# Delta stage of a two-layer AdaLN kernel: 48 projected columns spread over the heads, in place of 768

## The reference, cut to what matters

```
q, k, v = (x @ Wq), (x @ Wk), (x @ Wv)            # 16 heads x 16
beta = sigmoid(x @ Wbeta + b_beta)                 # one value per head
vsum = v.sum(-1)                                   # one value per head
h_t = beta_t * h_(t-1) + k_t * vsum_t              # per head, 16 values (all columns j of k alike in h)
o_t = q_t.sum(-1) * h_t                            # only the sum of q over a head matters
y = x + o @ Wo + b_o ;  out = ln_g * normalise(y) + ln_b
```

## Time and profile before

| | |
|---|---|
| median of 3 runs | 2445.0 us |
| the profiled execution | 2444.07 us |
| its span | 2442.4 us (1.67 us lie around it) |
| PE / DVE / ACT / POOL busy | 2070.8 / 1827.2 / 1274.5 / 700.0 us |
| `phase_delta`, first matmul to the first of the next phase | 1745.46 to 1932.10 us |

### The profile page before, as it was taken

One profiled execution on the slowest core, in us unless ns is written; L12 is line 12 of the kernel. 1 busy time (PEld: TensorE's weight loads), 2 busy tenths in 40 slices (PEclk: granted clock), 3 DMA queues, 4 the chain that ended last, 5 costly groups with the idle time before them and its releaser, 6 DMA issues. The chain is left out here.

```text
span 2442.4 us, 39942 instructions
## 1 busy us (share of the span) xinstructions
PE 2070.8 (85%) x10413; PEld 881.0 (36%) x10413; DVE 1827.2 (75%) x2427; ACT 1274.5 (52%) x1553; POOL 700.0 (29%) x1073
## 2 busy tenths in 40 slices
PE   5886888888889988888888889578799597999996
PEld 4441222222222122222222221456454254677775
DVE  2886999989999989999899999458589642333332
ACT  0555888878888878888788888122212210111110
POOL 0563111111111121111111111037356566133334
PEclk8898999999999999999999999789899798999998
DMA  3453221203121222212030000440000033344442
GB/s 118 131 173 98 38 36 20 28 12 50 20 30 18 28 43 39 29 20 28 24 82 19 15 3 0 142 148 30 1 0 0 6 110 118 98 105 101 106 95 26
DMA packets 124640, 133.71 MB, mean 55 GB/s; under 512 B 35258, under 2 KB 118931, under 8 KB 123793
## 3 DMA queue, kind: packets, MB, share of 16 engines
q1 hardware_dynamic: 109904, 117.96, 19.6%
q0 software_dynamic: 14592, 14.08, 3.1%
HBM read 96.95 MB, written 50.63 MB: 60 GB/s over the span
## 5 line engine op out<-in xcount | busy, mean ns | idle before, releaser
L914 DVE SCALAR_TENSOR_TENSOR arena<-ps_s,arena 128x1024 f32<-128x1024 f32 (+3 forms) x1152 | 1229.1, 1128 | 85.2 <-ACT arena L886 62.8
L886 ACT ACTIVATE arena<-ps_s 128x1024 f32<-128x1024 f32 (+3 forms) x1152 | 1043.3, 951 | 280.8 <-PE ps_s L792 266.3
L792 PE MATMUL ps_s<-arena 128*128 128x512 bf16 (+3 forms) x2304 | 645.4, 369 | 152.8 <-DVE arena L914 98.3
L817 PE MATMUL ps_o<-arena 128*32 128x512 f32 (+3 forms) x4608 | 578.2, 574 | 16.7 <-POOL arena L950 16.2
L792 PEld LDWEIGHTS ps_s<-arena 128*128 (+1 forms) x2304 | 174.2, 97 | 841.1 <-issue 709.2
L945 POOL COPY arena<-values 128x64 f32 x576 | 134.3, 236 | 878.6 <-PE ps_o L817 865.5
L1934 ACT ACTIVATE arena<-g_ps_g 128x320 f32<-128x320 f32 (+1 forms) x96 | 41.9, 436 | 315.6 <-PE g_ps_u L1866 315.6
L2130 POOL DMA_INDIRECT out<-values,slot_ids x80 | 123.4, 1542 | 247.4 <-DVE values L2081 215.6
L2054 DVE TENSOR_TENSOR arena<-g_ps_u,arena 128x320 f32<-128x320 f32 (+1 forms) x96 | 47.1, 491 | 165.3 <-ACT arena L1934 165.3
L817 PEld LDWEIGHTS ps_o<-arena 128*32 128x32 f32 x4608 | 91.2, 108 | 197.6 <-issue 144.7
L950 POOL TENSOR_SCALAR_AFFINE_SELECT arena<-arena 128x512 f32<-128x512 f32 x128 | 81.2, 634 | 241.8 <-DVE arena L914 241.8
(11 more groups left out here) (208 smaller groups left out, 1943.3 us busy)
## 6 DMA issues: line engine op xcount, KB each, us to landing
arena<-parts_dram SPq DMA_DIRECT2D x320, 64.0 KB, 3.0
parts_dram<-arena SPq DMA_DIRECT2D x32, 384.0 KB, 3.2
arena<-parts_dram SPq DMA_DIRECT2D x24, 512.0 KB, 7.1
slots_in_dram<-in_empty_slots SPq DMA_DIRECT2D x10, 1040.0 KB, 19.7
arena<-slots_in_dram SPq DMA_DIRECT2D x16, 650.0 KB, 5.9
arena<-in_L_ffn_w_gate SPq DMA_DIRECT2D x16, 352.0 KB, 3.1
arena<-in_L_ffn_w_up SPq DMA_DIRECT2D x16, 352.0 KB, 3.5
arena<-in_L_attn_x SPq DMA_DIRECT2D x8, 512.0 KB, 3.6
```

The lines of the kernel that those rows point to most:

```text
L792: last = pe.matmul(ps_s[:, (2 * step.slot + pair) % 3, h, step.w0:], m.k_stack[:, bass.ds(head, 1), bass.ds(step.kt * P, P)].rearrange("p ...
L817: last = pe.matmul(ps_o[32 * h:32 * h + 32, step.j % 2, step.w0:], v_pad[:, step.slot, h], probs[:, step.slot, h, step.w0:], start=step.fi ...
L886: act.activation(probs[:, step.slot, 2 * pair:2 * pair + 2, step.w0:], ps_s[:, (2 * step.slot + pair) % 3, :, step.w0:], ACT.Exp, scale=1. ...
L914: dve.scalar_tensor_tensor(p, ps_s[:, (2 * step.slot + pair) % 3, :, step.w0:], 0.0, p, ALU.not_equal, ALU.mult).then_inc(bank, 1)
```

## The change

In `phase_weights` the six copies over the columns go. Instead one narrow matrix `l1_narrow` of 96 columns is filled: v sums at 0 to 15, Wbeta at 32 to 47 (loaded there), q sums at 64 to 79, zeros between. A constant 0/1 matrix `spread`, loaded from memory, maps 16 heads to 256 channels, once in each group of 32 partitions. `b_beta` is loaded in another layout.

In `phase_delta` the narrow product is made once for a block, copied out by three ScalarE instructions on 32 partitions each (the middle one with the sigmoid), and spread to 128 channels by three matmuls of 32 rows each, at three row positions of the array, for each half. The products for the keys are as before. All of the scan's TensorE work moves one step later. The scan reads beta from PSUM. The second normalisation goes from VectorE to ScalarE, with GpSimd giving -mean/deviation as its offset.

```diff
@@ LayerNorm
+    def scale_and_offset(self, pool, b, s):
+        hold(self.m, pool, self.mvs, b + 1)
+        pool.tensor_scalar(self.ve[:, s], self.mv[:, s, :, 1], EPS, None, ALU.add).then_inc(self.added, 1)
+        pool.tensor_scalar(self.offset[:, s], self.mv[:, s, :, 0], -1.0, None, ALU.mult).then_inc(self.added, 1)
+        hold(self.m, pool, self.added, 2 * b + 2)
+        pool.tensor_tensor(self.rstd[:, s], self.ve[:, s], self.m.mhalf[:], ALU.pow).then_inc(self.rst, 1)
+        hold(self.m, pool, self.rst, 2 * b + 1)
+        pool.tensor_tensor(self.offset[:, s], self.offset[:, s], self.rstd[:, s], ALU.mult).then_inc(self.rst, 1)
+    def normalise_by_scale(self, act, b, s, tiles):
+        act.wait_ge(self.rst, 2 * b + 2)
+        for t in range(TT):
+            last = act.activation(self.xn[:, s, t], tiles[:, t], ACT.Identity, bias=self.offset[:, s, t:t + 1],
+                                  scale=self.rstd[:, s, t:t + 1])
+        last.then_inc(self.normed, 1)
@@ phase_weights
-            for n, w in enumerate((m.l1_q, m.l1_v)):
-                link(dve.tensor_reduce(sums[:, n], w.rearrange("p k (h d) -> p k h d", d=DH), AX.X, ALU.add))
-            for k in range(KC):
-                for src, w in ((sums[:, 0, k], m.l1_q), (sums[:, 1, k], m.l1_v), (m.beta_narrow[:, k], m.l1_beta)):
-                    dve.tensor_copy(w[:, k].rearrange("p (h d) -> p h d", d=DH),
-                                    src.rearrange("p (h a) -> p h a", a=1).to_broadcast([P, NH, DH]))
+            for at, w in ((64, m.l1_q), (0, m.l1_v)):
+                link(dve.tensor_reduce(m.l1_narrow[:, :, at:at + NH], w.rearrange("p k (h d) -> p k h d", d=DH), AX.X, ALU.add))
+                link(dve.memset(m.l1_narrow[:, :, at + NH:at + 32], 0.0))
+            link(dve.memset(m.l1_narrow[:, :, 32 + NH:64], 0.0))
@@ phase_delta, TensorE
+            def project_narrow(b, s, h):
+                pe.wait_ge(k_copied, 2 * b + 1)
+                for k in range(KC):
+                    last = pe.matmul(ps_k[0:96], m.l1_narrow[:, k], m.h_odd[:, k, bass.ds(b * BT, BT)], start=k == 0, stop=k == KC - 1)
+                last.then_inc(n_done, 1)
+            def project_keys(b, c):
+                if c == 0:
+                    pe.wait_ge(n_copied, 3 * b + 3)
+                else:
+                    pe.wait_ge(k_copied, 2 * b + 2)
...
+            def spread(b, c):
+                pe.wait_ge(n_copied, 3 * b + 3)
+                pe.wait_ge(q_used, 2 * b + c + 1)
+                for row, (ps, heads) in enumerate(((ps_v, narrow), (ps_b, decay), (ps_q, narrow))):
+                    at = 32 * row
+                    last = pe.matmul(ps[:, :], m.spread[at:at + 32, c], heads[at:at + 32], start=True, stop=True, tile_position=(at, 0))
+                last.then_inc(spread_done, 1)
-            pipeline(pe, [(0, lambda b, s, h: project(b, 0)), (1, out), (0, lambda b, s, h: project(b, 1)),
-                          (3, lambda b, s, h: ln2.transposes(pe, b, s))])
+            pipeline(pe, [(1, lambda b, s, h: project_keys(b, 0)), (1, lambda b, s, h: spread(b, 0)),
+                          (1, lambda b, s, h: project_keys(b, 1)), (2, out), (1, lambda b, s, h: spread(b, 1)),
+                          (0, project_narrow), (4, lambda b, s, h: ln2.transposes(pe, b, s))])
@@ ScalarE
+            def take_narrow(b, s, h):
+                act.wait_ge(n_done, b + 1)
+                act.wait_ge(spread_done, 2 * b)
+                act.activation(narrow[0:32], ps_k[0:32], ACT.Copy).then_inc(n_copied, 1)
+                act.activation(decay[32:64], ps_k[32:64], ACT.Sigmoid, bias=m.b_beta[32:64, 0:1]).then_inc(n_copied, 1)
+                act.activation(narrow[64:96], ps_k[64:96], ACT.Copy).then_inc(n_copied, 1)
-            pipeline(act, [(0, take), (3, modulate)])
+            def normalise(b, s, h):
+                act.wait_ge(ln2.turned, b + 1)
+                act.wait_ge(rows_done, b + 1)
+                ln2.normalise_by_scale(act, b, s, m.x[:, bass.ds(b * TT, TT)])
+            pipeline(act, [(0, take_narrow), (4, modulate), (0, lambda b, s, h: take(b, 0)), (0, lambda b, s, h: take(b, 1)),
+                           (2, normalise)])
@@ VectorE
-                dve.wait_ge(beta_made, n + 2)
-                dve.tensor_tensor_scan(state[:, c], beta[:, c], keys[:, c], start, ALU.mult, ALU.add).then_inc(scanned, 1)
+                dve.tensor_tensor_scan(state[:, c], ps_b[:, :], keys[:, c], start, ALU.mult, ALU.add).then_inc(scanned, 1)
-                           (1, lambda b, s, h: ln1.normalise(dve, b, s, y[s], out=y[s])), (2, normalise)])
+                           (1, lambda b, s, h: ln1.normalise(dve, b, s, y[s], out=y[s]))])
@@ GpSimd
-                            (2, lambda b, s, h: ln2.inverse_deviation(pool, b, s)), (1, gain), (2, rows)])
+                            (2, lambda b, s, h: ln2.scale_and_offset(pool, b, s)), (1, gain), (2, rows)])
```

More of the change, by code:

```diff
@@ L187, in place_weights @@
     a = Carver(m.arena)
-    (m.w_o, m.w_r, m.w_k, m.w_v, m.l1_k, m.l1_q, m.l1_v, m.l1_beta, m.l1_o) = (a.take(KC, D) for _ in range(9))
+    (m.w_o, m.w_r, m.w_k, m.w_v, m.l1_k, m.l1_q, m.l1_v, m.l1_o) = (a.take(KC, D) for _ in range(8))
+    m.l1_narrow = a.take(KC, 96)
+    m.spread = a.take(KC, P)
     m.router = a.take(KC, 32)
@@ L192, in place_weights @@
     m.mu = a.take(2, KC)
-    m.b_beta = a.take(KC)
+    m.b_beta = a.take(1)
     m.ln_gain, m.ln_shift, m.b_o = a.take(D), a.take(D), a.take(D)
     m.router_b = a.take(E_)
-    m.beta_narrow = a.take(KC, NH)
     m.even_at = a.at
@@ L216, in load_weights @@
     for dst, name in ((m.w_o, "woT"), (m.w_r, "W_rT"), (m.w_k, "W_kT"), (m.w_v, "W_vT"), (m.l1_k, "L1_attn_Wk"),
-                      (m.l1_q, "L1_attn_Wq"), (m.l1_v, "L1_attn_Wv"), (m.beta_narrow, "L1_attn_Wbeta"), (m.l1_o, "L1_attn_Wo"),
+                      (m.l1_q, "L1_attn_Wq"), (m.l1_v, "L1_attn_Wv"), (m.l1_narrow[:, :, 32:32 + NH], "L1_attn_Wbeta"), (m.l1_o, "L1_attn_Wo"),
                       (m.router, "router_wide"), (m.s_gate, "L1_ffn_sw_gate"), (m.s_up, "L1_ffn_sw_up")):
@@ L223, in load_weights @@
         load(m.mu[:, k], m.ins[name].rearrange("(k p) -> p k", p=P), allow_slow_non_contiguous=True)
-    load(m.b_beta, m.ins["b_beta_rep"].rearrange("(k p) -> p k", p=P), allow_slow_non_contiguous=True)
+    load(m.b_beta, m.ins["b_beta_narrow"].rearrange("(k p) -> p k", p=P), allow_slow_non_contiguous=True)
+    load(m.spread, m.ins["spread"].rearrange("p (k n) -> p k n", k=KC))
     for dst, name in ((m.ln_gain, "L1_attn_ln_g"), (m.ln_shift, "L1_attn_ln_b"), (m.b_o, "L1_attn_b_o"),
@@ L1157, in __init__ @@
         self.rstd = a.take(2, TT)
+        self.offset = a.take(2, TT)
         if own:
@@ L1209, in sem @@
             return ctx.enter_context(nc.semaphore("w_" + name))
-        sums = Carver(m.arena2).take(2, KC, NH)
         chain, zeroed = sem("chain"), sem("zeroed")
@@ L1509, in phase_delta @@
         keys = a.take(KC, BT)
-        beta = a.take(KC, BT)
+        narrow = a.take(BT)
+        decay = a.take(BT)
         state = a.take(KC, BT)
@@ L1519, in phase_delta @@
         ps_y = pb("ps_y", [P, 2, 2 * D])
-        k_done, v_done, b_done, q_done = sem("k_done"), sem("v_done"), sem("b_done"), sem("q_done")
-        k_copied, v_used, beta_made, q_used = sem("k_copied"), sem("v_used"), sem("beta_made"), sem("q_used")
+        n_done, k_done, spread_done = sem("n_done"), sem("k_done"), sem("spread_done")
+        n_copied, k_copied, v_used, q_used = sem("n_copied"), sem("k_copied"), sem("v_used"), sem("q_used")
         scanned, carried, y_done, y_added, scaled, gained = (sem("scanned"), sem("carried"), sem("y_done"), sem("y_added"),
@@ L1530, in _ @@
             pe.sem_inc(ln2.turned, 2)
[L1532 to L1541, removed]
+            def project_narrow(b, s, h):
[8 more added lines that the diff above has]
+                    pe.wait_ge(k_copied, 2 * b + 2)
+                for k in range(KC):
+                    last = pe.matmul(ps_k[:, :], m.l1_k[:, k, c * P:c * P + P], m.h_odd[:, k, bass.ds(b * BT, BT)],
+                                     start=k == 0, stop=k == KC - 1)
+                last.then_inc(k_done, 1)
+            def spread(b, c):
[5 more added lines that the diff above has]
+                last.then_inc(spread_done, 1)
             def out(b, s, h):
@@ L1559, in _, with take @@
             act.sem_inc(k_copied, 1)
-            act.sem_inc(beta_made, 1)
             act.sem_inc(ln2.taken, 1)
[L1563 to L1570, removed]
+            def take_narrow(b, s, h):
[4 more added lines that the diff above has]
+                act.activation(narrow[64:96], ps_k[64:96], ACT.Copy).then_inc(n_copied, 1)
+            def take(b, c):
+                n = 2 * b + c
+                act.wait_ge(k_done, n + 1)
+                act.wait_ge(scanned, n + 1)
+                act.activation(keys[:, c], ps_k[:, :], ACT.Copy).then_inc(k_copied, 1)
             def modulate(b, s, h):
```

(12 more changed lines are left out.)

## The result

| | before | changed |
|---|---|---|
| median of 6 runs | 2444.04 us (2441.87 to 2447.03) | 2459.28 us (2457.71 to 2464.45) |
| ratio, 95% interval | | 1.0066, 1.0053 to 1.0079 |
| span of the profiled execution | 2442.4 us | 2462.7 us |
| PE / DVE / ACT / POOL busy | 2070.8 / 1827.2 / 1274.5 / 700.0 | 2041.9 / 1784.2 / 1294.1 / 693.8 |
| R(2) to R(7), five periods | 98.2 us | 120.2 us |

R(t) is, as in the prediction, the start of the product with q (L1599, now L1639) of half 0 of block t. TensorE works 28.9 us less, VectorE 43.0 us less, and the kernel is slower. The forecast was 2461 in a range of 2446 to 2478. The profiled execution of the changed kernel is one of its slower ones, 5 us above the median (2464.45).

The account below looks back on a forecast made before the run. VectorE bounds the kernel by a little, TensorE right behind; changed, a ring of waits sets five periods of 23.9 us. +16.3 up to R(7), +0.6 behind it and -0.8 in `phase_weights` give +16.1: 2461 us, range 2446 to 2478.

Parts of the forecast that it names:

- the sum: Whole kernel: +16.3 us up to R(7), +0.6 behind it, -0.8 in `phase_weights`, together +16.1 us.
- DVE, R to the end of the statistics: Each period in `phase_delta`: product with q, residual, add and statistics on VectorE take 7.16 us.
- GpSimd and hand-over to ScalarE: Each period: GpSimd makes the normalisation's scale and offset in 2.30 us, plus 0.12 to hand over.
- PE to R at full clock: Each period on TensorE: keys 1.72, spread 1.07, keys 1.72, `out` to the product with q 3.72 us.
- the low clock: TensorE restarts at 1.2 GHz after waiting 8.7 us for ScalarE, costing 2.4 us in all five periods.
- start of the phase to R(0): Block 0: narrow product 3.54 at low clock, copies 1.69, keys 1.72, spread 1.07, then 2.10 us; R(0) = 1755.9.
- the ring: `phase_delta`, R(t) to R(t+1): one chain of waits over four engines, 21.48 us at full clock, 23.9 with restart.
- The rival in which the engines' loads decide: `phase_delta`: normalisation's inputs come early enough, each engine's own load decides, 2412 us; 12% chance.
- The normalisation and take_narrow on ScalarE: Each period: four normalisations of 0.56 less 0.09 overlap, 1.88 us; three copies of the narrow product, 1.69 us.
- The spread: TensorE, each half: three row tiles run side by side in 1.07 us, bounds 0.43 and 2.57.
- The serial rival: The spread's matmuls run one after the other, +1.5 us for each on the chain, 2476 us; 12% chance.
- The DVE: VectorE, each block: normalisation's 4.66 us go, scan 1.28 for 3.08; 19.63 falls to 13.2 us.

Follow-up runs that it names:

- run 5: Changed kernel with TensorE's pause filled from block 3 on by repeated narrow and throw-away products, transposes first: 2452.78 us, ratio 1.0035.
- run 1: Changed kernel with ScalarE's second normalisation one block later, skew 3 in place of 2: 2431.64 us, ratio 0.9957.
- run 2: Changed kernel with the second normalisation back on VectorE, all else as changed: 2431.95 us, ratio 0.9962.
- run 6: Changed kernel with ScalarE's normalisation and GpSimd's rows at skew 3, and `out` ahead of the second keys on TensorE: 2423.12 us, ratio 0.9911.
- run 4: Changed kernel with the narrow product computed five times over in every block: 2482.91 us, ratio 1.0170.

## Why the prediction was right, point by point

The mechanism was right; that the size came out so close is in part luck. The medians differ by 15.2 us (the ratio makes it 16) where the sum had +16.1. But in the profiled execution of the changed kernel, the only one whose terms can be read, the difference is 20.3 us. The terms are these.

| term | predicted | measured |
|---|---|---|
| DVE, R to the end of the statistics | 7.16 | 7.14 |
| GpSimd and hand-over to ScalarE | 2.42 | 2.48 |
| ACT normalise | 1.88 | 1.98 |
| ACT take_narrow, hand-over | 1.79 | 2.04 |
| PE to R at full clock | 8.23 | 8.46 |
| the low clock | 2.4 | 1.9 |
| period | 23.9 | 24.03 |
| start of the phase to R(0) | 10.4 | 13.7 |
| R(0) to R(2) | 27.7 | 30.8 |
| R(2) to R(7) | 119.5 | 120.2 |
| behind R(7) to the next phase | +0.6 against before | -0.3 |
| `phase_weights`, from its first product (L1226, now L1246) to the next phase | -0.8 | -0.7 (7.2 to 6.5) |

The measured parts of the period are the differences of starts in its timeline; full clock is what the keys (1.92) and the spread (1.06) take in run 5 and in the first periods, with 1.82 and 3.66 for the rest.

From the start of the phase to R(7) that is 164.7 us against 141.4 before, 23.3 more, where the sum had 16.3. With -0.3 and -0.7 it makes +22.3; all else in the kernel took 2.0 us less in this execution, for a reason that wasn't looked for, which gives the +20.3. Of the 7.0 us by which the sum was short up to R(7), the five periods of the ring are only 0.7. The rest lies in the first blocks, 3.3 up to R(0) and 3.1 from there to R(2). The two ends of the period's range, 22.6 and 26, aren't what its bounds add up to (22.2 and 26.7, the spread side by side); the measured period lies in either range.

*The ring.* Right in its mechanism and its members: runs 1 and 2 cut it at different places, and the time fell by 27 us in both; run 1 alters nothing but the order in ScalarE's queue. The rival in which the engines' loads decide is out: even with the ring cut, in run 1, another ring sets the period. Only in run 2 is it a load, VectorE's 17.8 us.

*The normalisation and take_narrow on ScalarE.* 1.98 and 1.89 against 1.88 and 1.69. One normalisation takes 0.59 us and not 0.56; the overlap of 0.09 that I took from L1200 is there (they start 0.50 apart). Among the three copies it is not: of 0.57, 0.68 and 0.59 us, they start 0.59 and 0.71 apart.

*The spread.* Three row tiles run side by side: six instructions in 1.06 us at full clock, 1.07 forecast. The serial rival is out.

*The clock.* It fell at every restart of the ring: the keys take 3.78 us in all five. The cost is 1.9 by the timeline (3.71 less 1.92 for the keys, 1.20 less 1.06 for the spread) and 2.0 by run 5, not 2.4: the level was back within the spread of the same block. So the restart came back in all five periods, as forecast. Where I was off is the start, here in the changed kernel (first three rows) and in run 2:

```profile
1743.29 3.70 PE L1554 MATMUL e_ps_k<-arena 128*96 128x512 f32 x4 [3.36 <-ACTq L1592]
1748.98 3.78 PE L1563 MATMUL e_ps_k<-arena 128*128 128x512 f32 x4 [1.99 <-ACT arena L1600]
1777.67 2.81 PE L1563 MATMUL e_ps_k<-arena 128*128 128x512 f32 x4 [1.99 <-ACT arena L1600]
1738.09 3.70 PE L1554 MATMUL e_ps_k<-arena 128*96 128x512 f32 x4 [3.36 <-ACTq L1592]
1743.78 1.99 PE L1563 MATMUL e_ps_k<-arena 128*128 128x512 f32 x4 [1.99 <-ACT arena L1600]
```

The narrow product of block 0 runs at the low level, as forecast. I counted the first keys behind it at full clock, and they ran low too, as did the first spread and the second keys (granted clock 0.50 to 0.51 up to 1758.30); the keys of block 2 ran partly so. In runs 1, 5 and 6, with the same first blocks, the first keys took 3.78 us as well, and R(0) came 13.6 us after the phase's start in run 1. In run 2 they took 1.99, and R(0) came after 10.9. That may be a part of why executions of the changed kernel lie up to 7 us apart: the traced execution with the fast start is the fastest of run 2, and those with the slow one are the slowest of the changed kernel and of runs 5 and 6 and the second slowest of run 1. But one execution of each was traced, so it is not shown, and why the median of the changed kernel lies 5 us under its profiled execution stays open.

*The DVE.* The scan reads beta from PSUM in 1.28 us, as taken. The relief of 6.5 us a block is real and worth nothing in this order. It pays in run 6: a period of 14.8 us would not be possible with VectorE's 19.6 us of work.

What I didn't see is the second ring, 16.7 us, which bounds any repair of the first; it changed nothing in the forecast, but it spoilt the expectation of run 1.

## What to carry to other kernels

Before moving work to an engine because it is idle, write down its queue in order and ask of each instruction behind the new one who needs it next: here a normalisation that waits for data of this step stood ahead of copies that feed TensorE, and ScalarE's wait of 12.5 us a block kept TensorE waiting for 8.9. When a change takes load off every engine, work out the chains of waits that lead from an instruction to itself one iteration later. The longest of them, if it is longer than every engine's load, is the period, and the next shorter one tells what a repair is worth (24.0 us here, then 16.7). One skew, (2, normalise) to (3, normalise), was the difference between 0.66% slower and 0.43% faster.

## What the runs showed of the hardware

- A pause of about 2 us was followed by the low clock in some places and not in others. In the changed kernel, behind stretches at 1.00 and 1.99 us of pause, the keys of block 1 took 1.99 us and those of block 2 2.81 (granted clock 0.64). In run 6 a pause of 2.27 us kept the level and one of 2.56 lost it (0.73 from there to the end of `out`); 1.30 us kept it in runs 1 and 6. The 8.8 to 9.8 us of the ring lost it each time. Filled with products on both sides (run 5) it stayed.
- In run 4 the clock fell (0.59 over the keys) with 1.92 us of pause and 1.04 us of transposes before it. By the Trainium skill, "TensorE: Matmul & The Clock Gate", "Part 4: PE-mode transpose", transposes don't count as TensorE being busy in the way that matmuls do. Counted from the last product the pause would then be 2.8 us. In runs 1 and 6 transposes and 1.30 us of pause kept the level, and run 5 has the transposes elsewhere but no pause either, so no run here shows the two apart.
- Keys followed by a spread take 1.92 us from start to start, keys followed by keys or by `out` 1.72 to 1.82: 0.1 to 0.2 us more, which I put down to the change between the full array and row tiles.
- ScalarE saves nothing by partitions: 32x512 takes 0.59 us, 128x512 0.60.
